# Loads of x from ScalarE's queue, both parts of p ahead of z, and x1 last in SyncE's queue

## The reference, cut to what matters

```python
q, k, v = split(x @ c_attn_w + c_attn_b)            # 16 heads of 16, one more key and value from cond
p = softmax(q @ k.T / 4 + causal mask)              # per sequence of 64 rows
y = (p @ v) @ c_proj_w + c_proj_b
q2, k2, v2 = relu(y @ Wq.T + bq), relu(y @ Wk.T + bk), y @ Wv.T + bv
out = q2 @ (k2.T @ v2) / (q2 @ sum(k2)) + y         # linear attention per sequence and head
x1 = x + layernorm(out) * gamma + beta
```

## Time and profile before

| | |
|---|---|
| median of 3 runs | 917.55 us |
| lowest and highest of them | 912.46 and 919.34 us |
| profiled execution, its own time | 920.51 us |
| its span in the trace | 918.8 us |
| busy in the span: TensorE (PE) | 753.5 us (82%) |
| VectorE (DVE) | 710.9 us (77%) |
| ScalarE (ACT) | 466.2 us (51%) |
| GpSimd (POOL) | 459.4 us (50%) |

### The profile page before, as it was taken

The page is one execution under the profiler, slowest core; times in us unless marked ns, Lnnn a source line. Parts: engine busy times, 40 slices in busy tenths (PEclk is TensorE's granted clock), DMA queues, the critical chain, the costliest instruction groups (busy, mean ns, idle before and its releaser), DMA issues.

```text
span 918.8 us, 23189 instructions
## 1 busy us (share of the span) xinstructions
PE 753.5 (82%) x7370; PEld 455.1 (50%) x7370; DVE 710.9 (77%) x1773; ACT 466.2 (51%) x1207; POOL 459.4 (50%) x596
## 2 busy tenths in 40 slices
PE   3336868788888888888767899999999999999965
PEld 2124545455555555555434455555555555555533
DVE  6077777777777777787553889999999999999983
ACT  2054656566777777777453444444444444444420
POOL 1045768877777777778630233333333333333342
PEclk9657878899999999999698999999999999999997
DMA  5865555677777777777501123332323333233333
GB/s 122 167 181 111 101 108 115 108 139 148 149 147 149 146 148 150 148 148 144 98 24 29 26 53 68 69 61 54 65 64 69 61 66 56 62 67 67 66 64 69
DMA packets 263438, 89.30 MB, mean 97 GB/s; under 512 B 233809, under 2 KB 262353, under 8 KB 263380
## 3 DMA queue, kind: packets, MB, share of 16 engines
q1 hardware_dynamic: 263380, 88.51, 48.5%
HBM read 25.45 MB, written 8.47 MB: 37 GB/s over the span
## 4 chain that ended last, share of the span: by engine, by line
DVE 27%; SPq 20%; issue 14%; PE 8%; ACT 4%; POOL 4%; DMA 3%; DVEq 1%; POOLq 0%; ACTq 0%
SPq L568 7%; SPq L541 5%; DVE fc L1511 4%; SPq L578 3%; PE bank L801 3%; DVE ffn_room L1577 3%; DVE prob L167 3%; DVE bank L164 3%; SPq L547 2%; DVE prob L171 2%; POOL xq L738 2%; DVE ffn_room L1569 2%; DVE ig L1513 1%; DVE bank L166 1%; DVE x_value L170 1%
## 5 line engine op out<-in xcount | busy, mean ns | idle before, releaser
L738 POOL TENSOR_TENSOR xq<-x_value,x_scale 128x256 f32<-128x256 f32 x32 | 29.4, 920 | 208.1 <-DVE x_value L171 208.1
L801 PE MATMUL bank<-gu,xqT 128*128 128x512 f16 (+1 forms) x576 | 127.3, 368 | 6.8 <-DMA xqT<-xq_split 6.8
L941 PE MATMUL bank<-wx,x1T 128*64 128x512 f16 x768 | 108.4, 406 | 8.1 <-DMA x1T<-x_split 7.5
L661 POOL TENSOR_TENSOR prob<-prob,row_max 128x520 f32<-128x520 f32 x64 | 73.7, 1152 | 74.7 <-DVE row_max L1393 74.2
L952 PE MATMUL bank<-wh,h 128*64 128x512 f16 x768 | 95.6, 385 | 0.7 <-ACT h L1215 0.7
L801 PEld LDWEIGHTS bank<-gu,xqT 128*128 128x128 f16 x576 | 56.0, 102 | 66.0 <-issue 13.2
L941 PEld LDWEIGHTS bank<-wx,x1T 128*64 128x64 f16 x768 | 73.8, 204 | 26.8 <-issue 8.2
L1030 PE MATMUL bank<-dn,hqT 128*128 128x256 f16 x576 | 70.3, 278 | 7.4 <-DMA hqT<-ffn_room 6.6
L668 POOL TENSOR_TENSOR p<-prob,p 128x512 f16<-128x512 f32 x64 | 71.6, 1119 | 2.2 <-ACT p L1112 2.2
L1030 PEld LDWEIGHTS bank<-dn,hqT 128*128 128x128 f16 x576 | 54.8, 99 | 26.3 <-issue 18.4
L759 POOL TENSOR_TENSOR ffn_room<-prob,h_fine 128x704 f16<-128x704 f32 x32 | 44.5, 1389 | 42.6 <-DVE h_rows L1522 42.6
(11 more groups left out here) (194 smaller groups left out, 1834.9 us busy)
## 6 DMA issues: line engine op xcount, KB each, us to landing
vimg_in<-image_values SPq DMA_DIRECT2D x64, 68.0 KB, 2.6
x_in<-in_x_columns SPq DMA_DIRECT2D x16, 256.0 KB, 3.0
x_res<-in_x SPq DMA_DIRECT2D x16, 256.0 KB, 3.1
x_rows<-x_rows_sb SPq DMA_DIRECT2D x32, 128.0 KB, 1.8
ffn_room<-x_rows SPq DMA_DIRECT2D x64, 64.0 KB, 2.2
out<-ffn_room SPq DMA_DIRECT2D x64, 64.0 KB, 2.0
add_mask<-in_mask_Bx1x1xS_ff SPq DMA_DIRECT2D x2, 512.0 KB, 7.5
qkT<-qk SPq DMA_TRANSPOSE x64, 4.2
```

What stands on the lines that cost most here:

```text
L661: pool.tensor_tensor(prob[:, r, :], prob[:, r, :], row_max[:, r, None].to_broadcast([P, 8, KEYS]), ALU.subtract).then_inc(s["shifted"], 1)
L738: pool.tensor_tensor(blocks(xq, D), blocks(fp4_x.value, D), spread(fp4_x.scale, D), ALU.mult).then_inc(s["xq_ready"], 1)
L801: last = pe.matmul(dst, lhs(a, c), rhs(b, c), start=first and c == 0 and a == b, stop=c == C - 1 and (a, b) == parts3[-1], skip_group_chec ...
L941: last = pe.matmul(bank[e][B * h:B * h + B, :], x1T16[m][:, c, :, at], half_cols(wx16, a, c, h), start=False, stop=True, skip_group_check= ...
```

## The change

SyncE's step now begins with the transposes of q and k; behind them come the first half of p, the image values, the second half of p, and last the transpose and the store of x1. The two loads from x leave SyncE for ScalarE, which issues them between the copy that makes `y_rows` and the one that makes the high part of `yT`; the load of `x_res` is now one of 128 rows in every step, with a semaphore for each parity, and the load of `x_in` stays one of 256 rows in every second step. On ScalarE the first high part of p comes right after `o_sum`, ahead of `neg_mean`, `offset`, `k2` and `v2`; the second exponential and the second high part of p come next, then `onT`, then `z_rows`. On GpSimd both low parts of p come ahead of `zg_rows`. The wait for `x1T_in` ahead of the high part of x1 stays as it is.

```diff
@@ SyncE
         def step(tiles):
-            t1, t2, _, t4, _, t6 = tiles
-            if t1 and (t1.loop is not None or t1.b > 0):
-                image_values(t1)
-            if t4 and t4.parity == 0:
-                after(sp, s["xb_ready"], t4.count(back=1))
-                sp.dma_start(x_res[:, :, :], x_pairs[t4.pair()]).then_inc(xres_loaded, 16)
-            if t1 and t1.parity == 0 and (t1.loop is not None or t1.b < NT - 2):
-
-                sp.wait_ge(s["xT_lo"], t1.count(2))
-                sp.dma_start(x_in[:, :, :], x_cols_pairs[t1.pair() + 1]).then_inc(x_loaded, 16)
+            t1, t2, _, _, _, t6 = tiles
             if t1:
 
                 hold(sp, s["qk_again"], t1.count(), "sp_passed")
...
+            if t2:
+                probs_turn(t2, 0)
+            if t1 and (t1.loop is not None or t1.b > 0):
+                image_values(t1)
+            if t2:
+                probs_turn(t2, 1)
             if t6:
                 hold(sp, s["x1_lo"], t6.count(), "sp_passed")
...
-            if t2:
-                probs_turn(t2, 0)
-                probs_turn(t2, 1)
@@ GpSimd
-            if t5:
-
-                pool.wait_ge(s["z_ready"], t5.count())
-                pool.tensor_tensor(zg_rows[:, :], z_rows[:, :], gamma_sb[:, :], ALU.mult).then_inc(s["zg_ready"], 1)
             if t2:
                 probs_lo(t2, 0)
                 image_part(t2, 1)
                 probs_lo(t2, 1)
+            if t5:
+
+                pool.wait_ge(s["z_ready"], t5.count())
+                pool.tensor_tensor(zg_rows[:, :], z_rows[:, :], gamma_sb[:, :], ALU.mult).then_inc(s["zg_ready"], 1)
...
-                pool.wait_ge(xres_loaded, t4.pair_count())
+                pool.wait_ge(xres_loaded[t4.parity], t4.pair_count())
@@ ScalarE
+            if t2:
+                probs_hi(t2, 0)
+            if t5:
+                act.wait_ge(s["mean_ready"], t5.count())
+                act.activation(neg_mean[:, :], mean_var[:, 0:1], ACT.Copy, scale=-1.0).then_inc(s["neg_ready"], 1)
...
             if t4:
                 act.wait_ge(s["kv2_ps"], t4.count())
...
+            if t2:
+                exp(t2, 1)
+                probs_hi(t2, 1)
+            if t3:
+                hi(t3, onT16[:, 0, :], bank[0][:, 0:D], "onT_ps", "onT_hi", "y_ps")
             if t5:
...
                 act.wait_ge(s["offset_ready"], t5.count())
...
-            if t2:
-                probs_hi(t2, 0)
-            if t3:
-                hi(t3, onT16[:, 0, :], bank[0][:, 0:D], "onT_ps", "onT_hi", "y_ps")
-            if t2:
-                exp(t2, 1)
             ffn_hi(t4, "outer")
-            if t2:
-                probs_hi(t2, 1)
...
+            if t1 and t1.parity == 0 and (t1.loop is not None or t1.b < NT - 2):
+
+                act.wait_ge(s["xT_lo"], t1.count(2))
+                act.dma_start(x_in[:, :, :], x_cols_pairs[t1.pair() + 1]).then_inc(x_loaded, 16)
+            if t3:
+                after(act, s["xb_ready"], t3.count(back=2))
+                act.dma_start(x_res[:, t3.parity, :], x_rows_tiles[t3.number()]).then_inc(xres_loaded[t3.parity], 16)
+            if t3:
                 hi(t3, yT16[:, 0, :], bank[6][:, D:2 * D], "yT_ps", "yT_hi", "kv2_ps")
```

More of the change, by code:

```diff
@@ L211, in program @@
     x_cols_pairs = x_columns.rearrange("(c p) (n r) -> n p c r", p=P, r=2 * P)
-    x_pairs = x.rearrange("b s d -> (b s) d").rearrange("(n j p) d -> n p j d", j=2, p=P)
+    x_rows_tiles = x.rearrange("b s d -> (b s) d").rearrange("(n p) d -> n p d", p=P)
     mask_sides = mask.rearrange("(n e) u v s -> e n (u v s)", e=2)
@@ L348, in program @@
     vimg_loaded = sem("vimg_loaded")
-    xres_loaded = sem("xres_loaded")
+    xres_loaded = [sem(f"xres_loaded{i}") for i in range(2)]
     hqT_in = [sem(f"hqT_in{i}") for i in range(2)]
@@ L1146, in step @@
                 act.copy(by_bank(o_sum[:, :, :]), o_part(1, HD)).then_inc(s["o_copied"], 1)
+            if t2:
[3 more added lines that the diff above has]
+                act.activation(neg_mean[:, :], mean_var[:, 0:1], ACT.Copy, scale=-1.0).then_inc(s["neg_ready"], 1)
+                act.wait_ge(s["neg_ready"], t5.count())
+                act.wait_ge(s["rstd_ready"], t5.count())
+                act.activation(offset[:, :], neg_mean[:, :], ACT.Copy, scale=rstd[:, 0:1]).then_inc(s["offset_ready"], 1)
             if t4:
```

## The result

| | before | after |
|---|---|---|
| median of 4 runs each | 917.44 us | 983.52 us |
| lowest and highest | 912.46 and 919.34 | 979.71 and 986.15 |
| profiled execution, its own time | 920.51 | 983.03 |
| its span in the trace | 918.8 | 981.3 |

The ratio is 1.0725 with a 95% interval of 1.0678 to 1.0772: the changed kernel is slower by 66 us in the medians, 62.5 us in the two profiled spans.

The account below looks back on a forecast made before the run. Prediction: SyncE's full queue bounds the kernel before; the change closes a 13.5 us ring. Loop +36.3 us, steps 30 and 31 +4.9, steps 5 to 9 +3, behind step 31 -1: 963.7 profiled, 961 median, range 940 to 984.

Parts of the forecast that it names:

- The bound of before: First stage of the kernel before: SyncE's queue never stands still, so its issues set the step, 11.54 us.
- The closed ring: Loop: x1T lands, ScalarE copies x1, x, q, k, SyncE issues qkT, pT, image, pT, next x1T; 13.5 us, chance 0.85.
- issue of x1T to start of the high part of x1: Ring's first term: the landing of x1's transpose, which ScalarE's copy awaits; 2.8 to 3.2 us, taken as 2.9.
- start of qkT to the first pT: Ring piece in SyncE's queue: issue of qkT, 3.2 us, and a gap of 0.3, before the first transpose of p.
- first pT to x1T: Ring piece in SyncE's queue: pT 1.24 us, image loads 1.2, pT 1.24, each with a gap of 0.3.
- both extra terms: SyncE's queue: pT behind qkT issues up to 0.6 us slower; first pT waits 0 to 1 us; 0.15 added together.
- I take nothing: ScalarE's 1.5 added load issues a step lie in its wait for TensorE's transpose of y; no cost counted.
- p ahead of z at no cost: GpSimd and ScalarE: the new order gives back most of 1.94 us to p; later z and x1_rows cost nothing.
- The other terms: Outside the loop: steps 30 and 31 +4.9 us, steps 5 to 9 +3, behind step 31 -1.
- x_in "late by up to 1 us" without cover: Load of x_in on ScalarE: without the longer x1T wait, late by up to 1 us in every second step.
- The queue as the bound: Rival: ring open, SyncE's issues set the loop's step at 10.86 us; 899.5 us in the profile, chance 0.05.
- The fallen clock: Rival: TensorE idles, drops to 1.2 GHz, 1.8 us more on the path of 22 steps; 1001 us, chance 0.08.

Follow-up runs that it names:

- b3: Kernel before with only p put ahead of z on ScalarE and GpSimd: 915.21 us, ratio 0.9984.
- b4: Kernel before with only a second buffer for the parts of x1: 917.34 us, ratio 1.0000.
- a3: Changed kernel with ScalarE's loads of x issued earlier, right behind the second high part of p: 967.42 us, ratio 1.0547.
- a1: Changed kernel with the transpose and store of x1 moved back to right behind the transposes of q and k: 936.25 us, ratio 1.0244.
- a2: Changed kernel with a second buffer for the parts of x1, SyncE's order kept: 928.68 us, ratio 1.0156.
- b1: Kernel before with only the transpose and store of x1 moved behind both transposes of p: 963.58 us, ratio 1.0518.
- b2: Kernel before with only the loads of x moved to ScalarE, at the place the change gives them: 925.00 us, ratio 1.0060.
- a5: Changed kernel with a second buffer for the parts of x1 and ScalarE's loads of x issued early: 908.59 us, ratio 0.9893.
- a7: a5 with the old order of p and z on ScalarE and GpSimd: 953.45 us, ratio 1.0395.

## Why the prediction was right, point by point

**The bound of before**, SyncE's queue at 11.54 us, holds: b3 and b4 change other things and give 11.55 and 11.57. One gap of the earlier trace rows is 0.20 us (311.63 to 311.83), under the 0.26 that I read as the least; nothing hangs on it.

**The closed ring** was the forecast, and it is what happened. Its four terms, as a mean of 15 steps from 236.9 to 448.75 us after:

| term | predicted | measured |
|---|---|---|
| issue of x1T to start of the high part of x1 | 2.9 | 3.12 |
| that to the start of qkT | 2.35 | 2.50 |
| start of qkT to the first pT | 3.65 | 3.86 |
| first pT to x1T | 4.6 | 4.66 |
| sum | 13.5 | 14.12 |

The sum meets the 14.10 us of a step between the issues of pT. The measured 983.52 us lies 0.5 us under the upper end of my range, 984, and one of the four executions (986.15) above it: that the ring would close was reasoned, that the time stayed inside the range was in part luck. The upper end of 14.3 us a step is not the sum that I called it either: 13.35 with both extra terms in full, 0.6 and 1.0, is 14.95.

**The size is what was off**: all four terms are above mine, and 20 steps of 0.6 us are 12.6 of the 19.3 us by which the profiled execution missed my 963.7. The first term carries a third of it. The step that failed is "issue of x1T to landing: 2.8 to 3.2, I take 2.9 us", a row of before, where x_in was issued 4.4 us ahead of x1T instead of 0.8 to 2.4. Of the cost of the issues on ScalarE I had written "I take nothing". They were free in ScalarE's time, which I did weigh, and not in the landing of the transpose beside them, which I did not: a3 took them away and the time from issue to copy fell to 2.5, the step by 0.48 us. The two extra terms that I named are both there: SyncE waited 0.4 us a step for p, which is the excess of the third term, and in every second step, those with the shorter wait, the first pT held the queue for 1.38 to 1.47 us instead of 1.24, which is in the fourth. I added 0.15 for both.

**p ahead of z at no cost** was right about z in this kernel: GpSimd's zg shows no wait left, and the low part follows the shift without a gap. These two rows answer to the earlier trace rows, where 1.94 us lay between them:

```profile
356.77 1.17 POOL L655 TENSOR_TENSOR prob<-prob,row_max 128x520 f32<-128x520 f32 x1
357.89 1.12 POOL L662 TENSOR_TENSOR p<-prob,p 128x512 f16<-128x512 f32 x1
```

I saw the road through GpSimd as an extra of 0 to 1 us on top of the ring; by the chain it is the longer of the two roads, 6.36 us from the high part of x1 to pT. My own rows gave 6.4 for it (6.9 less 0.5 of slack), and I took 6.0. One sign that I named failed: TensorE's waits for pT are not gone, they come to 13.9 us in 15 waits from 240 to 480 us after.

**The other terms**: steps 30 and 31 gave +5.0 (+4.9 predicted); steps up to 9 gave +6.8 where I took 3 from a range of 0 to 8; what follows step 31 gave +1.8 where I took -1 from -3 to +2. Most of the 6.8 us needs both the closed ring and the late loads: the first pT of step 9, at 189.2 us after, comes at 182.5 in a3, at 180.7 and 180.1 in a1 and a2, and at 185.0 in b1, against 182.3 before. What follows step 31 takes 476.1 to 483.5 us in the eleven other kernels, so 1.8 us there can't be told from nothing.

**x_in "late by up to 1 us" without cover**: the mechanism was right and it is what a1, a2 and b2 ran into, but where it decides it is 1.2 us in b2, 1.4 in a1 and 1.9 in a2, each every second step, and a1 and a2 came 24 us and more above my expectations, of which it is one part. In the changed kernel it costs nothing, as I had said, since the ring covers it.

**The rivals.** The queue as the bound (899.5) needed an open ring; when a2 opened it, x_in took over at 928.7, and only with the loads early as well did it come near, in a5 at 908.6. The step there is 11.20 us, not the 10.86 of SyncE's issues alone. The fallen clock (1001) is there in part:

```profile
371.41 0.72 PE L889 MATMUL bank<-v,k 64*128 64x130 f32 x8 [2.51 <-ACT v L1153]
...
372.84 1.32 PE L823 MATMUL bank<-attn,xT 128*64 128x256 f16 x12
```

After a wait of 2.51 us the products of L823 take 1.32 us, the level of 1.2 GHz for most of them, where 0.85 us is their time at 2.4 GHz in another step (the same at 356.40 after); at 274.39 and 288.49 they take the full 1.49. The granted clock from 240 to 420 us is 0.91 after and 1.00 before. But the chain's sum by line names no TensorE line, and a3, with 0.87 in the same stretch, has the shorter step. So in the changed kernel this falls in slack, which was my reason against it. Where the ring of x1 is open it doesn't: in a7 it is on the path, as shown above.

## What to carry to other kernels

Before an issue is moved down an in-order queue, look for who waits for its landing to reuse a buffer: if that engine then produces what the head of the same queue waits for, the two close a ring of one step, and its length (landing, copies, and all issues in between) is the new floor. A second buffer opens it, but so does leaving the issue early, and that costs nothing. Parts of a change are not additive: p ahead of z was worth 1.4 us alone, within what can be told from nothing, and 45 us with the rest, and each opened wait showed the next one below it, so the rows of the kernel before, where a wait is covered, give a lower end and not a value for what is late next.

## What the hardware showed that I had not expected

- A transpose's landing depends on what moves beside it: x1T to ScalarE's copy 3.60 us in steps with a load of x_in under way (3.15 to 3.36 where it was issued 2.4 us ahead, 3.61 to 4.40 at 0.8 to 1.2 us), 2.57 in the others; 2.4 to 2.7 to landing in every step of a3. x_in itself landed in 3.8 us after (median), 3.4 in a3, 3.0 in b2, all from ScalarE's queue, and in 3.0 from SyncE's before; so what moves beside it counts here, and not the queue.
- The issue of a load of x on ScalarE took 0.33 to 0.44 us after, with single ones up to 0.74 (SyncE before, in the loop: 0.40, with single ones up to 0.58). In the step shown above the one at 361.40 lies in a wait of ScalarE for TensorE.
- The same transpose of x1 held SyncE's queue for 1.84 us right behind those of q and k, 1.52 to 1.90 over the loop, and for 1.19 to 1.31 us in the loop where it came last.
- A fallen clock costs by where it falls. In the changed kernel it is 0.91 and off the path; in a7 it is 0.91 as well, and the steps with slow products for k2 and v2 are 1.2 us longer.
